# Recurrence stage: unread wide matmuls, a warm-up run of them, input products in four pieces, the square sum moved from ScalarE to VectorE

## The reference

```python
ms = jnp.mean(jnp.square(tokens), axis=-1, keepdims=True)
x = tokens * jax.lax.rsqrt(ms + EPS) * norm_w      # then [B, T, 16 heads, 16]
a_t = jnp.tanh(a)
def step(state, x_t):
    state = jnp.tanh(einsum('bhs,hst->bht', state, a_t) + einsum('bhd,hds->bhs', x_t, b))
    mixed = einsum('bhs,hsd->bhd', state, c) + skip[None] * x_t
    return (state, mixed)
_, outs = jax.lax.scan(step, state0, xs)            # 512 steps, one after the other
return tokens + outs @ w_out.T + b_out
```

## Time and profile before

| | us |
|---|---|
| median of 3 runs | 2884.94 |
| lowest, highest | 2883.08, 2890.91 |
| the profiled execution | 2887.34 |
| its span | 2885.3 |
| its mean granted clock | 0.825 |

### The profile page before, as it was taken

One profiled execution on the slowest core, in us unless ns is written; L12 is line 12 of the kernel. 1 busy time (PEld: TensorE's weight loads), 2 busy tenths in 40 slices (PEclk: granted clock), 3 DMA queues, 4 the chain that ended last, 5 costly groups with the idle time before them and its releaser, 6 DMA issues. The chain is left out here.

```text
span 2885.3 us, 89560 instructions
## 1 busy us (share of the span) xinstructions
PE 2670.6 (93%) x35096; PEld 1864.7 (65%) x35096; DVE 1763.2 (61%) x4998; ACT 1040.9 (36%) x2798; POOL 1039.5 (36%) x1346
## 2 busy tenths in 40 slices
PE   5899999999999999699999999899999999998897
PEld 2455555555555555466666666688888888886665
DVE  5667666666666677589999999222222222222798
ACT  1444444444444454333333333233333333332221
POOL 4334434343434344245555555222222222221222
PEclk8999999999999999999999999555555555555999
DMA  3001111111111111100000000000000000001122
GB/s 99 23 31 38 39 38 38 38 38 38 38 38 38 38 38 38 51 31 30 29 29 29 29 29 21 28 25 22 25 24 22 25 22 25 23 25 41 43 82 81
DMA packets 91569, 103.83 MB, mean 36 GB/s; under 512 B 8624, under 2 KB 78032, under 8 KB 91216
## 3 DMA queue, kind: packets, MB, share of 16 engines
q1 hardware_dynamic: 91216, 98.67, 10.7%
HBM read 48.31 MB, written 33.55 MB: 28 GB/s over the span
## 5 line engine op out<-in xcount | busy, mean ns | idle before, releaser
L1495 PEld LDWEIGHTS ps_state<-r_state,later_pairs_a 64*64 64x64 f32 x8176 | 480.0, 214 | 68.9 <-issue 51.7
L1498 PE MATMUL ps_state<-r_state,later_pairs_a 64*64 64x16 f32 x8176 | 515.0, 267 | 0.0
L1495 PE MATMUL ps_state<-r_state,later_pairs_a 64*64 64x16 f32 x8176 | 515.0, 267 | 0.0
L1498 PEld LDWEIGHTS ps_state<-r_state,later_pairs_a 64*64 64x64 f32 x8176 | 480.0, 214 | 0.0
L1426 ACT ACTIVATE r_state<-ps_state 128x64 f32<-128x64 f32 x1024 | 229.3, 224 | 567.7 <-PE ps_state L1498 564.0
L297 POOL TENSOR_SCALAR_AFFINE_SELECT probsT<-probsT 128x512 f32<-128x512 f32 x256 | 159.9, 637 | 678.6 <-ACT probsT L384 275.4
L401 DVE CUSTOM_DVE_ANT_0 ps_near<-ps_near,mask 128x512 f32<-128x512 f32 (+1 forms) x512 | 270.5, 591 | 145.7 <-PE ps_near L502 145.2
L401 DVE CUSTOM_DVE_ANT_0 ps_far<-ps_far,mask 128x384 f32<-128x384 f32 (+1 forms) x512 | 198.6, 460 | 124.0 <-PE ps_far L502 124.0
L1452 DVE TENSOR_SCALAR r_xT<-ps_state,later_recurrence_columns 128x128 f32<-128x128 f32 x128 | 39.1, 347 | 308.7 <-PE ps_state L1543 308.7
L1234 PE MATMUL ps_down<-kept_w_downT,f_hT 128*128 128x256 f32 (+1 forms) x768 | 200.7, 390 | 1.9 <-ACT f_hT L1108 1.9
L510 PE MATMUL ps_far<-Q,K 32*128 32x256 f32 (+2 forms) x1536 | 180.4, 411 | 1.9 <-ACT probsT L384 0.5
(11 more groups left out here) (208 smaller groups left out, 5655.7 us busy)
## 6 DMA issues: line engine op xcount, KB each, us to landing
k_swap<-k_sin SPq DMA_DIRECT2D x128, 128.0 KB, 2.1
xT<-in_xT_dram SPq DMA_DIRECT2D x16, 512.0 KB, 3.9
xtok<-in_x_dram SPq DMA_DIRECT2D x16, 512.0 KB, 3.9
x_rows<-x SPq DMA_DIRECT2D x16, 512.0 KB, 2.9
f_x<-x_rows SPq DMA_DIRECT2D x64, 128.0 KB, 2.0
x_rows<-f_x SPq DMA_DIRECT2D x64, 128.0 KB, 1.7
r_x<-x_rows SPq DMA_DIRECT2D x64, 128.0 KB, 2.1
x_rows<-r_x SPq DMA_DIRECT2D x64, 128.0 KB, 2.0
```

The lines of the kernel that those rows point to most:

```text
L1495: nc.tensor.matmul(sums[half(v), j % 2, stays, c, now], A[half(v), 3 * q, c, :], state[half(v), (j - (t == 0)) % 2, stays, c, before], sta ...
L1498: out = nc.tensor.matmul(sums[half(1 - v), j % 2, changes, c, now], A[half(v), 3 * q + 1 + was, c, :], state[half(v), (j - (t == 0)) % 2, ...
```

## The change

- `fill(j, bank, columns, times, start)` is new: matmuls over the full array whose result nobody reads, w_outT against w_outT, written into `room` (`TURN`, or `OUT` for the first tile). In a tile of the steady part there is one of 256 columns at positions 0, 9, 11, 13 and 15, and one of 128 columns at position 3.
- Before the first tile, 9 of 256 columns stand ahead of the first transposes, and one ahead of each piece of the first `feed`.
- The transposes move from position 1 to 3. `mix` is split: chunk 0 stays at 1, chunk 1 goes to 2. The projection is split over positions 5 and 7 (`project`; fills stand in for it in tile 0). `feed` is split into four pieces by chunk and parity at 9, 11, 13 and 15.
- The Square on ACT goes. DVE computes mean and variance of x with bn_stats and bn_aggr at the head of its step, and POOL forms mean squared plus variance plus epsilon: three small operations before the power instead of one. The factor on norm_w goes too.

The core of the diff:

```diff
+                        pool.wait_ge(x_mv_ready, i + 3)
+                        nc.gpsimd.tensor_tensor(ms[:, s:s + 1], x_mv[:, s, 0:1], x_mv[:, s, 0:1], ALU.mult).then_inc(squared, 1)
+                        pool.wait_ge(squared, i + 3)
+                        nc.gpsimd.tensor_tensor(ms[:, s:s + 1], ms[:, s:s + 1], x_mv[:, s, 1:2], ALU.add).then_inc(ms_ready, 1)
...
-                        if t == 0 and exists(i, 2):
...
-                            nc.scalar.activation(square[:, j % 2, :], x[:, (j + 2) % UNROLL, :], ACT.Square,
-                                                 accum_out=ssq[:, j % 2:j % 2 + 1]).then_inc(ssq_ready, 1)
...
+                    if exists(i, 2):
+                        dve.wait_ge(x_loaded[(j + 2) % UNROLL], 16 * k + 16 * ((j + 2) // UNROLL + 1))
+                        if later(i, 2, 2):
+
+                            dve.wait_ge(ms_ready, 2 * i + 1)
+                        nc.vector.bn_stats(x_stats[:, j % 2, :], x[:, (j + 2) % UNROLL, :])
+                        dve.drain()
+                        nc.vector.bn_aggr(x_mv[:, j % 2, :], x_stats[:, j % 2, :]).then_inc(x_mv_ready, 1)
...
+                def fill(j, bank, columns, times, start):
+                    for n in range(times):
+                        nc.tensor.matmul(room[:, (j + 1) % 2, bank, 0:columns], w_outT[:, 0, 0:P], w_outT[:, 1, 0:columns],
+                                         start=start, stop=True, skip_group_check=True)
...
+                            if at == 0 and exists(i, 0):
+                                fill(j, TURN, DIM, 1, True)
+                            if at in (1, 2) and exists(i, -1):
+                                c = at - 1
...
+                                mix(j, c).then_inc(mix_full, 1)
+                            if at == 3 and exists(i, 0):
+                                fill(j, TURN, P, 1, True)
+                            if at == 3 and exists(i, 1):
+                                if i == -1:
+                                    fill(j, OUT, DIM, 9, True)
                                 pe.wait_ge(xn_ready, i + 2)
...
+                            if at in (5, 7) and exists(i, 0):
+                                c = (at - 5) // 2
+                                if i == 0:
+                                    fill(j, OUT, DIM, 1, True)
+                                else:
+                                    project(i, j, c)
...
+                            if at in (9, 11, 13, 15) and exists(i, 1):
+                                n = (at - 9) // 2
...
+                                out = feed(j, n // 2, n % 2)
+                                if n == 3:
+                                    out.then_inc(inputs_in, 1)
+                            if at in (9, 11, 13, 15) and exists(i, 0):
+                                fill(j, TURN, DIM, 1, False)
```

More of the change, by code:

```diff
@@ L1307, in recurrence @@
         x = sb("x", [P, UNROLL, DIM])
-        square = sb("square", [P, 2, DIM])
-        ssq = sb("ssq", [P, 2])
+        x_stats = sb("x_stats", [P, 2, 6])
+        x_mv = sb("x_mv", [P, 2, 2])
         ms = sb("ms", [P, 2])
@@ L1501, in recur, with feed @@
                     out.then_inc(summed[q], 1)
-                def feed(j, c):
+                def feed(j, c, parity):
                     s = (j + 1) % 2
[L1507 to L1517, removed]
-                    return out
+                    for v in range(2):
+                        for bank in range(BANKS):
+                            rows = slice(32 * bank, 32 * bank + 32)
+                            xT_now = xT[rows, (j + 1) % UNROLL, c, :]
+                            if bank % 2:
+                                out = nc.tensor.matmul(steps_of(sums[half(v ^ parity), s, bank, c, :], parity), B[rows, 2 * c + v, :], steps_of(xT_now, parity),
+                                                       start=(c == 0 and parity == 0), stop=False, skip_group_check=True)
+                            elif parity == 0:
+                                nc.tensor.matmul(sums[half(v), s, bank, c, :], B[rows, 2 * c + v, :], xT_now,
+                                                 start=(c == 0), stop=False, skip_group_check=True)
+                    return out
@@ new lines, in project @@
+                def project(i, j, c):
+                    s = (j - 1) % 2
+                    pe.wait_ge(outs_ready, 2 * i + (c - 1))
+                    out = nc.tensor.matmul(room[:, s, OUT, :], outs[:, s, c, :], w_outT[:, c, :], start=(c == 0), stop=(c == CC - 1))
+                    if c == CC - 1:
+                        out.then_inc(out_full, 1)
+                def fill(j, bank, columns, times, start):
+                    for n in range(times):
+                        nc.tensor.matmul(room[:, (j + 1) % 2, bank, 0:columns], w_outT[:, 0, 0:P], w_outT[:, 1, 0:columns],
+                                         start=start, stop=True, skip_group_check=True)
@@ L1539, in step @@
                             s = (j - 1) % 2
-                            if at == 1 and exists(i, 1):
+                            if at == 0 and exists(i, 0):
+                                fill(j, TURN, DIM, 1, True)
+                            if at in (1, 2) and exists(i, -1):
+                                c = at - 1
+                                if c == 0:
+                                    for side in range(SIDES):
+                                        pe.wait_ge(state_ready[side], i * STEPS)
+                                mix(j, c).then_inc(mix_full, 1)
[4 more added lines that the diff above has]
+                                    fill(j, OUT, DIM, 9, True)
                                 pe.wait_ge(xn_ready, i + 2)
@@ new lines, in step @@
+                            if at in (5, 7) and i == TILES:
+                                project(i, j, (at - 5) // 2)
+                            if at in (9, 11, 13, 15) and exists(i, 1):
+                                n = (at - 9) // 2
+                                if i == -1:
+                                    fill(j, OUT, DIM, 1, n == 0)
+                                if n == 0:
+                                    pe.wait_ge(xT_ready, i + 2)
+                                    if exists(i, -1):
+                                        pe.wait_ge(z_added, i)
+                                out = feed(j, n // 2, n % 2)
+                                if n == 3:
+                                    out.then_inc(inputs_in, 1)
```

17 lines of the change are left out of this document (5 added, 12 removed).

## The result

The changed kernel takes 2868.07 us in the median (2857.12 to 2872.33, 7 runs), the kernel before 2886.91 (2881.66 to 2899.95, 7 runs, same chip). The ratio is 0.9926, 95% interval 0.9909 to 0.9943: 0.74% faster, 19 us. The prediction said 2833 us, 52 us faster. The profiled execution took 2869.42 us with a span of 2867.7, and its mean granted clock is 0.969 (before 0.825).

A forecast was written before the change was run, and what follows sets the result against it. At 1.2 GHz chain and PE are nearly even; at full clock PE bounds. Tile 12.0 for 12.89 us: 2887.34 - 63 x 0.89 + 4 = 2835, less 2.4 for the profiled execution, 2833 us; range 2765 to 2900.

The forecast's parts named there:

- The clock: Recurrence stage: TensorE's clock rises with the warm-up and stays at 1.00; clock up and PE bound given 0.77.
- rival 1: Recurrence stage: the clock falls or never rises, a tile takes 20.6 us, all tiles about 3370 us; chance 0.17.
- The place named as the thinnest: About 3.4 us around the 0.6 us wait in every tile, with little full-array work, where the clock might fall.
- two stretches of other layers: 913.1 to 916.5, busy 3.28 us, nearly all 32-row shapes: clock fell; 1029.1 to 1032.5, 1.44 us full-array: clock stayed.
- The sum: Per tile on PE at full clock: pieces 11.3 us, waits 0.6 and 0.05, together 12.0 us against 12.89.
- halve: `recur` to `recur` on PE goes from 0.447 to 0.22 us at full clock; its 0.36 to the last pass halves.
- its upper bound: Top of the range, 2900 us, made with group spacing 0.06 us and tails of 0.12 us.
- The wait: Position 5 of each tile: PE waits 0.6 us for the first `outs`, since DVE does both xT chunks first.
- rival 2: Recurrence stage: small passes don't gain from the clock, group spacing stays 0.107 us, tile 14.4 us, 2985 us; chance 0.05.
- The chain: Each time step: the chain through tanh takes 0.73 us at full clock; every step is longer, so tanh is covered.
- the Square: Its move off ACT, which isn't the bound, to statistics on DVE and POOL was said to cost nothing.
- the start: Before the steady tiles: 9 warm-up fills and four in the first `feed` add 4 us, between 2 and 7.

## Why the prediction came out as it did

**The clock**, the step with the most risk, was right. It rose with the warm-up and stayed at 1.00 through the stage, and rival 1's price for a stage at the low clock, 3370 us, came to 21 us of the run without warm-up (3391; a tile is 20.8 us there, 20.6 in the rival). The place named as the thinnest, around the wait, didn't bring it down. That the clock could be lost in this mix was seen rightly too, but the argument, from two stretches of other layers, named no amount: 1024 columns in the second half of the tile held in all four runs, 512 in none.

**The sum** failed, in its terms for the small passes and the tails. The wide pieces, which had rows at full clock, were right within 0.01 us. The terms without such a row were all too low, and they decide the miss, 19 us gained for 52 forecast: `recur` with the tail behind it 0.58 for 0.535, a single one 0.35 for 0.315, mix 0.36 for 0.32, and the feed pieces 0.40 and 0.28 for 0.335 and 0.23. The step that failed is "halve", taking `recur` at 0.22 and its three spacings at half of 0.36: the spacing of the groups does nearly halve, 0.107 to 0.058, but the first group behind another shape takes 0.08, so that a `recur` takes 0.25 us (2210.21 - 2209.96) and its last group starts 0.20 behind its first. The tail shrinks less than supposed: from the start of the last group to the next shape it is 2206.24 - 2206.09 = 0.15 us now, where 0.135 was taken (0.20 at 1.2 GHz). (The wide pass's tail that the 0.135 goes by is 0.163 in its own rows, 0.379 - 0.216, not 0.166; that moves nothing.) An error of 0.03 to 0.07 us each looks small, but there are 16 of them in a tile and 63 tiles: 45 us, of which the shorter wait takes 10 back. The range, 2765 to 2900, holds 2868, but its upper bound was made with tails of 0.12 us; measured as the sum's 0.135 is, the tail is 0.15, above that bound. The spacing, 0.058, is within its 0.06.

**The wait** at position 5 was right in place, cause and sign, and 0.16 us too long: from the transposes' end (2207.99 + 0.38) to the projection it is 0.96 us, where 1.08 was taken, since the first xT chunk starts only 0.53 us before the first `outs` chunk now (0.64 in the earlier trace rows), and the two `recur` in between take 0.58 for 0.535. `z` ahead of the first feed piece costs 0.10 us (0.04).

**The small passes gain from the clock** (rival 2 is out). Sixteen passes take 0.25 us, 16 ns each, and starts in different quarters stand 0.01 us apart at full clock too (2205.89 and 2205.90 in the timeline). The floor of about 25 ns between starts that the Trainium skill gives ("TensorE: Matmul & The Clock Gate", Wait — 56ns, not 53.3ns?) is no floor over tiles in different quarters of the array here; the measurement decides.

**The chain** of tanh stayed covered everywhere, **the Square** cost and brought nothing, and the start was 3 us later (first `recur` at 1830.2 against 1827.4), 4 in the sum. That agreement shows little: without any warm-up it came at 1832.2 in one profile and at 1826.5 in another.

What the prediction didn't ask is what the change could do without. Its own working had the fills at 3.6 us of a tile and called them not hidden; the wait it found is one of order. Step by step, `outs` first is worth 25 us, leaving out the fills at positions 0 and 3 another 63, and the undivided `feed` 38: 2742 us, 5% under the kernel before, with the clock as steady as in the changed kernel in all five runs. Fewer unread columns still go lower (2725), but no longer in every run. Whether the old order of work, with the warm-up and with fills put into it, would hold the clock as well was not run; at the low clock the new order alone costs 89 us, so that rival to the change stays open.

## What to carry to other kernels

A piece that changes the array's tile shape costs a tail at either clock (0.20 us from the last group to the next shape at 1.2 GHz, 0.15 at 2.4), and its passes may be free beside others of their shape on other rows of the array (0.27 us alone, 0.01 in company): count the changes of shape as well as the passes, and put pieces of one shape together. When unread matmuls are to hold the clock, find by runs how few do it, look at every run and not the median, and keep a margin: in all four profiled losses the clock did not come back before the stage's end, and a kernel that went on with its unread matmuls at the low clock was slower than one without any (3037 and 3048 against 2974). An operation in an in-order queue belongs behind the one whose reader comes sooner, however early its own input is there.

## What the runs showed of the hardware

- TensorE at the low clock with PE busy without a gap does not rise by itself: 200.00 of 200 us busy at 0.50 in one kernel, 199.88 with 1408 unread columns per tile in another. The Trainium skill says that the gate follows how busy TensorE has been of late ("TensorE: Matmul & The Clock Gate", What's actually happening). Here the profile's busy share is no measure for it: what raised the clock was a run of nothing but full-array matmuls, and what lost it a mix that was busy all the same.
- At full clock a matmul row of 64 rows, 64 columns of weights and 16 moving columns is 206 ns long (264 at 1.2 GHz) and its weight load 135 (223): of the row, only a part follows the clock.
- PE has short pauses of 0.15 to 0.55 us, not at the same place in any two of these kernels' profiles, which end in nothing that the profile shows. All 14 of them fell while the clock was 1.00 and in kernels with 640 or fewer unread columns per tile.
